# Attention between two expert layers: one stack of keys for both passes, fewer scratch transfers, and another order of the work beside the passes

## Chip, cores and metric

One core of a Trainium2 chip runs the whole program as one launch. The metric is the device time in microseconds. TensorE (PE) multiplies matrices, VectorE (DVE), ScalarE (ACT) and GpSimd (POOL) work on tiles, and SyncE (SP) issues the transfers (DMA) between SBUF and DRAM. Each engine works through its own instructions in order and meets the others at semaphores.

## The reference, cut to what matters

Sixteen sequences of 512 rows and 128 features go through three layers: half of a top-2-of-8 expert layer, attention, half of the expert layer again. Only attention changes.

```python
def attention(x):                       # x: layer norm of the stream, [16, 512, 128]
    q, k, v = ((x @ W + b).reshape(16, 512, 16, 8) for W, b in ((Wq, bq), (Wk, bk), (Wv, bv)))
    scores = einsum('bthd,bshd->bhts', q, k) / sqrt(8)
    scores += slope[h] * -abs(s - t)     # alibi
    scores = where(s > t, -inf, scores)  # causal
    out = einsum('bhts,bshd->bthd', softmax(scores), v)
    return out.reshape(16, 512, 128) @ Wo + bo
```

## The kernel before

`macaron` runs `moe_layer`, `attention` and `moe_layer` one after the other, with the stream x resident in SBUF.

**Steps, groups and units.** In `attention` every engine runs `step(b)` for b from -3 to 16, and each step is a `walk` over 4 groups g of 11 units n, written (g, n) here. A step works on several sequences at once. In each unit TensorE makes scores of sequence b+1 for its row maxima (`take_max_scores`, units 0 to 10, L895 and L898), and transposed scores of sequence b for the exponentials (`take_exp_scores`, units 0 to 9, L917). VectorE reduces the former (L1104), ScalarE exponentiates the latter (L997), POOL masks the diagonal blocks (L1069), and after the units of `PV_AFTER` TensorE multiplies the values with the group before (`weigh_values`, L933). Both kinds of scores go through rings of 3 PSUM tiles, so that TensorE is at most three units ahead of VectorE and of ScalarE.

**Side work.** `SIDE_WORK` says after which unit TensorE puts a piece in that is needed once a sequence: `turn_h` (transposes of the normalised rows, of b+2), `project_q` and `project_k` (of b+2), `project_v` (of b+1), `shift_lo` and `shift_hi` (a transpose of the maxima), `turn_o0`, `turn_o1`, `turn_o` and `output`. All go through one PSUM tile, `side_ps`, so each waits until ScalarE or VectorE has read the piece before it. `PREPARE` places the rest: POOL's `split_q0` to `split_k3`, which take q and k apart into three bf16 parts, the layer norm's statistics, and the normalisation of b+3.

**The stacks.** One matmul with a height of up to 64 rows yields a score in full precision. It wants a stack: for each pair of heads, 6 products of parts x 8 features = 48 rows, then constant rows (3 for alibi; `FINE` rows, which mask inside a diagonal block of the maxima; a `FAR` row, which masks in the exponentials; a `SHIFT` row, which subtracts the row's maximum there). The even heads lie in partitions 0 to 63, the odd ones in 64 to 127, and a unit's two matmuls use one half each. There are a stack of q (`q_st`) and two of k (`k_max`, `k_exp`), which differ in their constant rows alone; each is doubled by the parity of the sequence.

**SyncE's order** in step b is written out in its `step`: `place_shift(b, 1)` puts the high half of the shift into `q_st`; `store_parts(b+2)` writes the parts to `scratch` in DRAM, a transfer for each of 6 products of q and of k (L835); `stack(b+2, 0)` waits until all of them have landed (L842) and half of the exponentials of b are made (L844), and reads the first half of the pairs back, for three stacks and two sides (L849); `place_shift(b+1, 0)`; and `stack(b+2, 1)`, which waits for the last exponentials of b. TensorE waits for the first half before unit (0, 0) of the maxima of the next step, and for the second before (2, 0); and for the shift's halves (L859) before (0, 0) and (2, 0) of the exponentials. Scratch holds a part as

```python
scratch = [parity, side, 6 products, 2 (even, odd head), HD, PAIRS, S]   # bf16, 128 KB a product
sp.dma_start(scratch[par, side, term].rearrange("u d r s -> r (u d) s"), parts[side][:, part])
```

The steps up to 1 and from 12 on are unrolled; those between are a loop of two.

## Time and profile before

| | |
|---|---|
| median of 3 runs | 1024.37 us (1023.14 to 1026.57) |
| the profiled execution's own time | 1028.07 us |
| its span, first to last instruction | 1026.4 us |
| granted TensorE clock, mean | 0.898 of 2.4 GHz |
| busy: PE, DVE, ACT, POOL | 844.9, 746.9, 639.1, 537.0 us |
| attention, from its first to its last matmul | about 171 to 861 us |

The profile is of one execution. An engine's busy time does not count its waits; a matmul's end is modelled, and matmuls overlap. A row of the windows gives each engine's busy time in one stretch, the granted clock (1.00 is 2.4 GHz, 0.50 is 1.2), the mean share of 16 DMA engines that were busy, and GB/s. A row of the timeline gives start, duration, instruction, and in brackets how long the engine was idle before it and what ended that.

### The profile page before, as it was taken

To read this page: it belongs to the slowest core of one execution; us is meant where nothing else is said; L and a number is where in the kernel's file an instruction comes from. 1 tells how busy PE (TensorE), PEld (TensorE's weight loads), DVE (VectorE), ACT (ScalarE), POOL (GpSimd) and SP (SyncE) were. 2 spreads that over 40 slices of the span, in tenths; PEclk is the share of its full clock that TensorE was granted. 3 is DMA by queue.
4 is the path that set the end of the run, shared out by engine and by line. 5 is a ranking of instruction groups with operands and counts; after the bars stand their busy time and mean duration, and the time that the engine had idled before them with its cause. 6 is when DMAs were issued, how large, how long until landed. Compare 5 with 4: busy or idle time off the path is not lost. (4 is left out here: it accounts for less than half of the span.)

```text
span 1026.4 us, 24158 instructions
## 1 busy us (share of the span) xinstructions
PE 844.9 (82%) x6498; PEld 397.3 (39%) x6498; DVE 746.9 (73%) x2534; ACT 639.1 (62%) x1538; POOL 537.0 (52%) x838
## 2 busy tenths in 40 slices
PE   4999996198898898799788878988987985999997
PEld 3444442043343343334334434433433423544443
DVE  4899995278686776767767866876866902899996
ACT  2767674106576676676666766776765773676765
POOL 3777775234364463553552643653643331677777
PEclk9999998557898898988988989989988997999999
DMA  6600000332322322322323223223223000011001
GB/s 164 99 0 0 0 0 1 106 124 96 137 77 87 137 78 91 121 95 92 108 87 113 96 86 126 87 87 134 84 83 134 13 1 21 12 31 31 23 29 42
DMA packets 61436, 75.25 MB, mean 73 GB/s; under 512 B 8084, under 2 KB 51988, under 8 KB 61204
## 3 DMA queue, kind: packets, MB, share of 16 engines
q1 hardware_dynamic: 61384, 74.61, 22.5%
q8 instruction: 26, 0.43, 0.2%
q14 instruction: 26, 0.21, 0.1%
HBM read 44.97 MB, written 29.36 MB: 72 GB/s over the span
## 5 line engine op out<-in xcount | busy, mean ns | idle before, releaser
L1104 DVE TENSOR_REDUCE att_neg_max<-att_max 128x1 bf16<-128x512 f32 (+3 forms) x704 | 411.5, 636 | 171.5 <-PE att_max L898 169.8
L997 ACT ACTIVATE att_probs<-att_exp 128x512 f32<-128x512 f32 x640 | 349.4, 598 | 188.3 <-PE att_exp L917 184.8
L1069 POOL TENSOR_SCALAR_AFFINE_SELECT att_probs<-att_probs 128x512 f32<-128x512 f32 x256 | 157.4, 637 | 316.8 <-ACT att_probs L997 316.8
L895 PE MATMUL att_max<-att_k_max,att_q_st 51*128 51x384 bf16 (+2 forms) x768 | 191.1, 300 | 99.3 <-DMA att_k_exp<-qk_parts 78.0
L917 PE MATMUL att_exp<-att_q_st,att_k_exp 64*128 64x512 bf16 (+3 forms) x1024 | 217.4, 321 | 4.0 <-DMA att_q_st<-att_shift 2.1
L933 PE MATMUL att_pv<-att_probs,att_v 128*32 128x512 f32 (+3 forms) x2048 | 207.2, 478 | 15.8 <-POOL att_probs L1069 15.8
L358 ACT ACTIVATE moe_scaled<-moe_hi,moe_gates 128x128 f32<-128x128 f32 x512 | 146.1, 372 | 61.2 <-PE moe_hi L304 60.9
L895 PEld LDWEIGHTS att_max<-att_k_max,att_q_st 51*128 51x128 bf16 x768 | 73.8, 98 | 281.6 <-DVE att_neg_max L1104 148.4
L898 PE MATMUL att_max<-att_k_max,att_q_st 62*128 62x128 bf16 x1024 | 178.2, 231 | 0.0
L518 DVE SCALAR_TENSOR_TENSOR x<-moe_lo,moe_gates,x 128x128 f32 (+1 forms) x512 | 160.6, 338 | 20.1 <-PE moe_lo L298 18.9
L298 PE MATMUL moe_lo<-moe_we,moe_hT 128*128 128x512 f32 x256 | 136.0, 613 | 0.0
L304 PE MATMUL moe_hi<-moe_we,moe_hT 128*128 128x512 f32 x256 | 135.2, 610 | 0.0
L395 POOL TENSOR_TENSOR moe_part<-moe_scaled 128x256 f32<-128x256 f32 x128 | 93.4, 730 | 55.3 <-ACT moe_scaled L358 50.2
L898 PEld LDWEIGHTS att_max<-att_k_max,att_q_st 62*128 62x128 bf16 x1024 | 90.5, 99 | 12.0 <-issue 11.7
L917 PEld LDWEIGHTS att_exp<-att_q_st,att_k_exp 64*128 64x128 bf16 x1024 | 70.5, 96 | 25.9 <-ACT att_probs L997 14.5
L933 PEld LDWEIGHTS att_pv<-att_probs,att_v 128*32 128x32 f32 x2048 | 42.1, 111 | 71.3 <-issue 48.3
L304 PEld LDWEIGHTS moe_hi<-moe_we,moe_hT 128*128 128x128 f32 x256 | 47.1, 193 | 48.5 <-issue 48.5
L409 POOL TENSOR_TENSOR x<-x,moe_part 128x128 f32 (+1 forms) x128 | 58.8, 460 | 12.6 <-DVE x L518 12.4
L336 ACT ACTIVATE moe_hn<-x,moe_nmr,moe_rstd 128x128 f32 (+1 forms) x128 | 52.7, 498 | 17.5 <-DVE moe_nmr L452 17.5
L402 POOL TENSOR_TENSOR moe_part<-moe_part 128x128 f32<-128x128 f32 x128 | 58.5, 457 | 0.2
L298 PEld LDWEIGHTS moe_lo<-moe_we,moe_hT 128*128 128x128 f32 x256 | 44.9, 195 | 33.1 <-issue 24.9
L388 POOL TENSOR_TENSOR moe_rstd<-moe_veps,f_consts 128x4 f32<-128x4 f32 x32 | 32.6, 1020 | 37.8 <-DVE moe_veps L447 35.8
(81 smaller groups left out, 879.1 us busy)
## 6 DMA issues: line engine op xcount, KB each, us to landing
qk_parts<-att_parts SPq DMA_DIRECT2D x192, 128.0 KB
att_q_st<-qk_parts SPq DMA_DIRECT2D x64, 192.0 KB
att_k_max<-qk_parts SPq DMA_DIRECT2D x64, 192.0 KB
att_k_exp<-qk_parts SPq DMA_DIRECT2D x64, 192.0 KB
x<-in_L_attn_x SPq DMA_DIRECT2D x16, 256.0 KB, 2.9
out<-x SPq DMA_DIRECT2D x16, 256.0 KB, 2.3
moe_we<-in_L_ffn_We SPq DMA_DIRECT2D x2, 512.0 KB, 4.7
att_q_st<-att_shift SPq DMA_DIRECT2D x64, 4.0 KB, 2.1
```

The lines of the kernel that those rows point to most:

```text
L298: nc.tensor.matmul(lo_ps[t][:], hT[par][:, t * P:(t + 1) * P], we[:, 0:HE, :], start=True, stop=True).then_inc(lo_out, 1)
L304: nc.tensor.matmul(hi_ps[t % 2][:], hT[par][:, t * P:(t + 1) * P], we[:, HE:E, :], start=True, stop=True).then_inc(hi_out, 1)
L358: ins = nc.scalar.activation(scaled[t % 2][:, e, :], hi_ps[t % 2][:, e, :], ACT.Copy, scale=gates[par][:, t, HE + e:HE + e + 1])
L395: nc.gpsimd.tensor_tensor(part2[t % 2][:], scaled[t % 2][:, 0:2, :], scaled[t % 2][:, 2:4, :], ALU.add).then_inc(part_step, 1)
L518: nc.vector.scalar_tensor_tensor(out=xt(b, t), in0=lo_ps[t][:, e, :], scalar=gates[par][:, t, e:e + 1], in1=xt(b, t), op0=ALU.mult, op1=AL ...
L895: nc.tensor.matmul(max_ps[m % RING][:, at:at + width - P], q_st[par][low:low + FINE_ROW, r, i * P:(i + 1) * P], k_max[par][low:low + FINE_ ...
L898: mm = nc.tensor.matmul(max_ps[m % RING][:, at + width - P:at + width], q_st[par][low:low + FAR_ROW, r, i * P:(i + 1) * P], k_max[par][low ...
L917: mm = nc.tensor.matmul(exp_ps[m % RING][:, c:c + S - j * P], k_exp[par][low:low + SIDE, r, j * P:(j + 1) * P], q_st[par][low:low + SIDE, ...
L933: mm = nc.tensor.matmul(pv_ps[VW * hh:VW * (hh + 1), j * P:S], v[par][:, j, 4 * half_at + hh, ab, :], probs[g % 2][:, n, c:c + S - j * P], ...
L997: nc.scalar.activation(probs[g % 2][:, n, :], exp_ps[m % RING][:], ACT.Exp).then_inc(exp_done, 1)
L1069: nc.gpsimd.affine_select(out=view, in_=view, compare_op=ALU.is_ge, fill=0.0, base=0, pattern=[[0, 4], [1, P]], channel_multiplier=-1).the ...
L1104: nc.vector.tensor_reduce(neg_max[par][:, g // 2, 1 - g % 2, heads[0]:heads[0] + len(heads), i], max_ps[m % RING][:, 0:len(heads) * width] ...
```

## The change

- One stack of k, `k_st`, takes the place of `k_max` and `k_exp`. Its constant rows are reordered (alibi, far, shift, fine). The maxima's diagonal blocks use all 64 rows, their other blocks the first 51; the exponentials use the first 53.
- Because the maxima now also see the shift row of `q_st`, `stack` writes zeros there (`no_shift`, 8 KB) before the shift is known, once for each half.
- Products that share a part are stored by one transfer, which reads the part 2 or 3 times: three transfers for q and three for k. The columns of Wq, bq, Wk and bk are put in the order (even or odd, feature, pair) on the host, so that a part's 128 partitions are one contiguous block of `scratch`.
- A half of the shift, for both sides of `q_st`, is placed by one transfer.
- `stack` waits for the store of q before q's transfers and for the store of k before k's.
- `SIDE_WORK` and `PREPARE` are laid out anew: q and k are projected and split in group 0 and at the head of group 1; the statistics and most of the normalisation stand in group 2 (`NORMALISE`), and `turn_h` transposes sequence b+3 at (3, 8), where before b+2 was transposed at (0, 3) of the next step.

```diff
@@ -30,16 +30,17 @@
-K_PARTS = [0, 1, 2, 0, 1, 0]
+K_PARTS = [1, 0, 2, 0, 1, 0]
+PART_TERMS = [[slice(0, 3), slice(3, 5), slice(5, 6)], [slice(1, 6, 2), slice(0, 5, 4), slice(2, 3)]]
...
-FINE_ROW = ALIBI_ROW + 3
+FAR_ROW = ALIBI_ROW + 3
+SHIFT_ROW = FAR_ROW + 1
+FINE_ROW = SHIFT_ROW + 1
...
-FAR_ROW = FINE_ROW + FINES
-SHIFT_ROW = FAR_ROW + 1
...
-assert SHIFT_ROW + 1 == SIDE
+assert FINE_ROW + FINES == SIDE
@@ -108,20 +109,21 @@
-        self.k_max_rows, self.k_exp_rows = [], []
+        fine_at, far_at = FINE_ROW - ALIBI_ROW, FAR_ROW - ALIBI_ROW
+        self.k_rows = []
...
+            rows[far_at] = bf16_parts(k_far, 1)[0]
...
-            rows[FAR_ROW - ALIBI_ROW] = bf16_parts(k_far, 1)[0]
-            self.k_exp_rows.append(nc.inline_tensor(rows, f"k_exp_rows_{ab}").ap().bitcast(BF16))
-            rows = rows[:FAR_ROW - ALIBI_ROW].copy()
-            rows[3:] = bf16_parts(k_fine, 1)[0][:, None]
-            self.k_max_rows.append(nc.inline_tensor(rows, f"k_max_rows_{ab}").ap().bitcast(BF16))
-        rows = np.full((SHIFT_ROW - ALIBI_ROW, PAIRS, S), one, np.uint16)
-        rows[FINE_ROW - ALIBI_ROW:FAR_ROW - ALIBI_ROW] = bf16_parts(q_fine, 1)[0][:, None]
-        rows[FAR_ROW - ALIBI_ROW] = bf16_parts(q_far, 1)[0]
+            rows[fine_at:] = bf16_parts(k_fine, 1)[0][:, None]
+            self.k_rows.append(nc.inline_tensor(rows, f"k_rows_{ab}").ap().bitcast(BF16))
+        rows = np.full((SIDE - ALIBI_ROW, PAIRS, S), one, np.uint16)
+        rows[far_at] = bf16_parts(q_far, 1)[0]
+        rows[SHIFT_ROW - ALIBI_ROW] = 0
+        rows[fine_at:] = bf16_parts(q_fine, 1)[0][:, None]
...
+        self.no_shift = nc.inline_tensor(np.zeros((2, PAIRS // 2, S), np.uint16), "no_shift").ap().bitcast(BF16)
@@ -562,17 +564,17 @@
-    {3: "turn_h", 7: "project_q"},
-    {0: "project_k", 5: "shift_hi", 9: "turn_o1"},
-    {3: "turn_o", 7: "shift_lo"},
-    {0: "project_v", 4: "output", 9: "turn_o0"},
+    {2: "project_q", 4: "shift_hi", 8: "project_k"},
+    {1: "turn_o1", 6: "project_v"},
+    {1: "turn_o", 6: "shift_lo", 10: "output"},
+    {1: "turn_o0", 8: "turn_h"},
...
-PREPARE = {(0, 10): "split_q0", (1, 0): "split_q1", (1, 1): "split_q2", (1, 2): "split_q3",
-           (1, 3): "split_k0", (1, 4): "split_k1", (1, 5): "split_k2", (1, 6): "split_k3", (2, 4): "add_bias",
-           (3, 0): "statistics", (3, 1): "aggregate", (3, 2): "add_eps", (3, 3): "take_root", (3, 6): "shift_mean",
-           (3, 7): "normalise0", (3, 8): "normalise1", (3, 9): "normalise2", (3, 10): "normalise3"}
+PREPARE = {(0, 5): "split_q0", (0, 6): "split_q1", (0, 7): "split_q2", (0, 8): "split_q3",
+           (0, 10): "split_k0", (1, 0): "split_k1", (1, 1): "split_k2", (1, 2): "split_k3", (2, 5): "add_bias"}
+NORMALISE = {(2, 0): "statistics", (2, 1): "aggregate", (2, 2): "add_eps", (2, 3): "take_root", (2, 7): "shift_mean",
+             (2, 8): "normalise0", (2, 9): "normalise1", (2, 10): "normalise2", (3, 0): "normalise3"}
@@ -712,9 +710,9 @@
-        SCRATCH_DMAS = len(Q_PARTS)
-        STACK_DMAS = 6
-        SHIFT_DMAS = 2
+        SCRATCH_DMAS = 3
+        STACK_DMAS = 5
+        SHIFT_DMAS = 1
@@ -784,11 +779,10 @@
                         on_exp(b, par, half, g, n)
-                    if on_prepare and (g, n) in PREPARE:
-                        if g < GROUPS - 1 and there(b + 2):
-                            on_prepare(b + 2, par, half + 1, PREPARE[g, n])
-                        if g == GROUPS - 1 and there(b + 3):
-                            on_prepare(b + 3, 1 - par, half + par + 1, PREPARE[g, n])
+                    if on_prepare and (g, n) in PREPARE and there(b + 2):
+                        on_prepare(b + 2, par, half + 1, PREPARE[g, n])
+                    if on_prepare and (g, n) in NORMALISE and there(b + 3):
+                        on_prepare(b + 3, 1 - par, half + par + 1, NORMALISE[g, n])
@@ -828,36 +822,32 @@
-                which = (Q_PARTS, K_PARTS)[side]
-                for term in sorted(range(len(which)), key=lambda t: which[t]):
-                    part = which[term]
+                for part, terms in enumerate(PART_TERMS[side]):
                     sp.wait_ge(split_step[side], b * 4 + (1, 3, 4)[part])
-                    sp.dma_start(scratch[par, side, term].rearrange("u d r s -> r (u d) s"),
-                                 parts[side][:, part]).then_inc(scratch_in[par][side], DMA)
+                    dst = scratch[par, side, terms].rearrange("t u d r s -> (u d r) t s")
+                    sp.dma_start(dst, parts[side][:, part].unsqueeze(1).to_broadcast(list(dst.shape))).then_inc(
+                        scratch_in[par][side], DMA)
...
-                if hf == 0:
-                    for side in range(2):
-                        sp.wait_ge(scratch_in[par][side], half * (SCRATCH_DMAS * DMA) + SCRATCH_DMAS * DMA)
+                pairs = slice(hf * PAIRS // 2, (hf + 1) * PAIRS // 2)
                 if after(b, 1):
                     sp.wait_ge(exp_out, (b - 2) * NE + (hf + 1) * NE // 2)
-                pairs = slice(hf * PAIRS // 2, (hf + 1) * PAIRS // 2)
-                for side, stacks in ((0, (q_st,)), (1, (k_max, k_exp))):
-                    for dst in stacks:
-                        for ab in range(2):
-                            sp.dma_start(dst[par][ab * SIDE:ab * SIDE + HEAD_ROWS, pairs, :],
-                                         scratch[par, side, :, ab, :, pairs]).then_inc(
-                                stack_in[par][hf], DMA)
+                sp.dma_start(q_st[par][SHIFT_ROW:SHIFT_ROW + SIDE + 1:SIDE, pairs, :],
+                             consts.no_shift).then_inc(stack_in[par][hf], DMA)
+                for side, dst in enumerate((q_st[par], k_st[par])):
+                    if hf == 0:
+                        sp.wait_ge(scratch_in[par][side], half * (SCRATCH_DMAS * DMA) + SCRATCH_DMAS * DMA)
+                    for ab in range(2):
+                        sp.dma_start(dst[ab * SIDE:ab * SIDE + HEAD_ROWS, pairs, :],
+                                     scratch[par, side, :, ab, :, pairs]).then_inc(stack_in[par][hf], DMA)
...
                 pairs = slice(hf * PAIRS // 2, (hf + 1) * PAIRS // 2)
-                for ab in range(2):
-                    rows = PAIRS // 2 * T
-                    sp.dma_start(q_st[par][ab * SIDE + SHIFT_ROW:ab * SIDE + SHIFT_ROW + 1, pairs, :],
-                                 shift[ab * rows:(ab + 1) * rows, :]).then_inc(shift_in[par][hf], DMA)
+                sp.dma_start(q_st[par][SHIFT_ROW:SHIFT_ROW + SIDE + 1:SIDE, pairs, :],
+                             shift[:]).then_inc(shift_in[par][hf], DMA)
@@ -893,11 +883,11 @@
                         nc.tensor.matmul(max_ps[m % RING][:, at:at + width - P],
-                                         q_st[par][low:low + FINE_ROW, r, i * P:(i + 1) * P],
-                                         k_max[par][low:low + FINE_ROW, r, 0:width - P], start=True, stop=True)
+                                         q_st[par][low:low + FAR_ROW, r, i * P:(i + 1) * P],
+                                         k_st[par][low:low + FAR_ROW, r, 0:width - P], start=True, stop=True)
                     mm = nc.tensor.matmul(max_ps[m % RING][:, at + width - P:at + width],
-                                          q_st[par][low:low + FAR_ROW, r, i * P:(i + 1) * P],
-                                          k_max[par][low:low + FAR_ROW, r, width - P:width], start=True, stop=True)
+                                          q_st[par][low:low + SIDE, r, i * P:(i + 1) * P],
+                                          k_st[par][low:low + SIDE, r, width - P:width], start=True, stop=True)
@@ -915,8 +905,8 @@
                     mm = nc.tensor.matmul(exp_ps[m % RING][:, c:c + S - j * P],
-                                          k_exp[par][low:low + SIDE, r, j * P:(j + 1) * P],
-                                          q_st[par][low:low + SIDE, r, j * P:S], start=True, stop=True)
+                                          k_st[par][low:low + FINE_ROW, r, j * P:(j + 1) * P],
+                                          q_st[par][low:low + FINE_ROW, r, j * P:S], start=True, stop=True)
@@ -1013,7 +1003,7 @@
-                    nc.scalar.activation(hT[par][:], side_ps[:], ACT.Copy).then_inc(side_read, 1)
+                    nc.scalar.activation(hT[1 - par][:], side_ps[:], ACT.Copy).then_inc(side_read, 1)
@@ -1040,7 +1030,7 @@
                     if after(b, 0):
-                        act.wait_ge(turned, use(b - 3, "turn_h"))
+                        act.wait_ge(turned, use(b - 4, "turn_h"))
@@ -1187,6 +1177,10 @@
+    for n in ("Wq", "bq", "Wk", "bk"):
+        a = arrays[f"in_L0_attn_{n}"]
+        by_side = a.reshape(-1, PAIRS, 2, HD).transpose(0, 2, 3, 1)
+        arrays[f"in_L0_attn_{n}"] = np.ascontiguousarray(by_side).reshape(a.shape)
```

## Rows read from the trace of the kernel before

**Rows 1.** Windows by step: the columns are each engine's busy time, PEclk, DMA share, GB/s

```profile
206.60:238.00 31.40, 28.64 (x129) 13.12 (x129) 26.47 (x55) 3.88 (x8) 9.33 (x10) 0.50 0.36 125
238.00:275.70 37.70, 30.29 (x295) 13.29 (x296) 27.62 (x57) 25.06 (x50) 19.07 (x26) 0.86 0.31 108
275.70:315.70 40.00, 33.12 (x343) 14.82 (x344) 28.96 (x60) 26.59 (x52) 19.06 (x26) 0.88 0.29 99
...
749.80:790.20 40.40, 33.35 (x342) 14.73 (x342) 27.97 (x50) 25.19 (x48) 18.00 (x25) 0.88 0.29 97
790.20:821.00 30.80, 29.21 (x330) 12.94 (x330) 26.35 (x47) 23.17 (x45) 8.86 (x15) 0.94 0.10 37
```

**Rows 2.** The waits, whole span: us in total, times, longest us

```profile
PE att_max L895 <- DMA att_k_exp<-qk_parts: 78.0, 16, 23.1
```

**Rows 3.** Timeline of TensorE: start, us, instruction, [idle before it and what ended it]

```profile
473.41 0.49 PE L895 MATMUL att_max<-att_k_max,att_q_st 51*128 51x384 bf16 x1 [2.11 <-DMA att_k_exp<-qk_parts]
...
495.28 1.06 PE L933 MATMUL att_pv<-att_probs,att_v 128*32 128x512 f32 x8 [0.91 <-POOL att_probs L1069]
...
836.05 0.82 PE L917 MATMUL att_exp<-att_q_st,att_k_exp 64*128 64x512 bf16 x3 [2.06 <-DMA att_q_st<-att_shift]
```

**Rows 4.** Timeline of SyncE's DMA queue in the prologue and one step

```profile
194.66 1.56 SPq L849 DMA_DIRECT2D att_q_st<-qk_parts  x2
...
449.23 1.20 SPq L859 DMA_DIRECT2D att_q_st<-att_shift  x2
450.56 8.08 SPq L835 DMA_DIRECT2D qk_parts<-att_parts  x12
462.00 1.52 SPq L849 DMA_DIRECT2D att_q_st<-qk_parts  x2
...
470.10 1.54 SPq L849 DMA_DIRECT2D att_q_st<-qk_parts  x2
```

**Rows 5.** Windows in which stores move (first) and stacks move (second)

```profile
183.50:192.50 9.00, 0.06 (x1) 0.00 (x0) 5.38 (x14) 1.78 (x4) 4.79 (x5) 0.50 0.51 165
...
464.00:480.50 16.50, 13.96 (x121) 5.88 (x116) 11.84 (x29) 9.96 (x20) 4.15 (x6) 0.79 0.38 140
```

**Rows 6.** Windows by group: two of the step from 434.9, three of the next

```profile
444.30:451.50 7.20, 7.20 (x82) 3.08 (x79) 6.64 (x12) 6.79 (x14) 6.20 (x8) 1.00 0.01 1
451.50:461.90 10.40, 8.59 (x89) 3.45 (x85) 6.70 (x14) 5.91 (x13) 6.31 (x10) 0.84 0.47 151
...
473.40:484.60 11.20, 11.19 (x86) 4.61 (x87) 5.96 (x11) 6.90 (x13) 1.99 (x4) 0.70 0.23 90
...
492.30:500.70 8.40, 6.95 (x81) 3.31 (x82) 6.31 (x12) 6.17 (x14) 6.15 (x9) 1.00 0.52 171
500.70:514.20 13.50, 8.20 (x94) 4.40 (x92) 9.65 (x26) 6.94 (x15) 3.93 (x6) 0.87 0.30 102
```

**Rows 7.** Timeline of TensorE: side work in the step from 434.9

```profile
444.72 1.12 PE L948 MATMUL att_side<-att_hT,att_wk 128*128 128x512 f32 x2
...
450.58 0.66 PE L972 MATMUL att_side<-f_consts,att_oT 128*128 128x128 f32 x4
...
462.31 1.16 PE L952 MATMUL att_side<-att_wv,att_hT 128*128 128x128 f32 x8
```

**Rows 8.** Part 5 of the page

```profile
L1104 DVE TENSOR_REDUCE att_neg_max<-att_max 128x1 bf16<-128x512 f32 (+3 forms) x704 | 411.5, 636 | 171.5 <-PE att_max L898 169.8
```

**Rows 9.** Timeline of VectorE: k's last split, the statistics

```profile
187.86 0.69 DVE L824 TENSOR_TENSOR att_parts<-att_rest,att_parts 128x512 bf16<-128x512 f32 x1
...
501.59 0.86 DVE L1115 BATCH_NORM_STATS2 att_bn<-x 128x6 f32 x4
```

**Rows 10.** Timeline of POOL: the splits and four masks

```profile
485.07 0.62 POOL L814 TENSOR_SCALAR att_parts<-att_qk 128x512 bf16<-128x512 f32 x1
485.77 1.16 POOL L817 TENSOR_TENSOR att_rest<-att_qk,att_parts 128x512 f32<-128x512 f32 x1
...
493.42 2.40 POOL L1069 TENSOR_SCALAR_AFFINE_SELECT att_probs<-att_probs 128x512 f32<-128x512 f32 x4
```

More of the change, by code:

```diff
@@ L620, in __init__ @@
         self.v_set = ctx.enter_context(nc.semaphore("att_v_set"))
[L621 removed]
+        self.N_WEIGHTS, self.N_ROWS, self.N_V = 8 * DMA, 8 * DMA, 6
     def load(self, eng):
@@ L743, in attention @@
         L = len(order)
-        before = {-2: 0}
-        for n in range(-1, 3):
-            before[n] = before[n - 1] + sum(present(n - 1, what) for what in order)
-        before[NSEQ - 2] = before[2] + (NSEQ - 4) * L
-        for n in range(NSEQ - 1, NSEQ + 2):
+        before = {-3: 0}
+        for n in range(-2, NSEQ + 2):
             before[n] = before[n - 1] + sum(present(n - 1, what) for what in order)
@@ L753, in use @@
             here = order[:order.index(what) + 1]
-            if isinstance(b, int) and b in before:
+            if isinstance(b, int):
                 return before[b] + sum(present(b, w) for w in here)
```

17 lines of the change are left out of this document (6 added, 11 removed).

## The prediction

> **What bounds the kernel now.** I read the page first, then the windows by step, the waits, SyncE's queue, and last the four groups inside one step. The page gives attention some 650 of 1026 us. The windows cut it into the steps that TensorE walks [rows 1]: in each, the maxima of sequence b+1, the exponentials of b and the values of b are interleaved. Thirteen steps in steady state run from 275.7 to 790.2, that is 39.6 us each, of which VectorE is busy 29, ScalarE 26.6, POOL 19. No engine fills a step.
>
> The waits say where the rest goes. TensorE stands at the first maximum of a step until the stack has come from DRAM: 16 times, 78.0 us together, the longest 23.1 [rows 2]. The 23.1 is the prologue; the other 15 are 54.9 us, 3.7 a step. Behind each such wait the clock is at its lower level: the first group after it runs 11.2 us at a granted 0.70, while a group with no wait in it takes 7.2 us at 1.00, all of it busy [rows 3, 6]. The group before it holds two more losses: TensorE stands 0.91 us for POOL's masks [rows 3], and the fourth group takes 8.6 us before the wait even starts, because VectorE has 9.65 us of work there and may lag by three units at most [rows 6].
>
> Why the stack is late is to be read in SyncE's queue [rows 4]. In the step that begins at 434.9 the stores of sequence b+2 are issued at 450.6, because they stand behind the shift's placement (449.2), and that behind a transpose scheduled in the second group. Twelve stores; the stack's first transfer goes out only when all have landed, at 462.0; its six transfers arrive at 473.4, 38.5 us after the step's start. While stacks move, the DMA engines are busy for 0.38 of 16 and move 140 GB/s, stores 0.51 and 165 GB/s [rows 5]: a stack transfer of 192 KB takes 1.4 us, and nothing issued faster helps it.
>
> **The change part by part.**
>
> *The chain of transfers.* project_q goes from (group 0, unit 7) to (0, 2), project_k from (1, 0) to (0, 8), the shift from (1, 5) to (0, 4), the splits from (0, 10)..(1, 6) to (0, 5)..(1, 2). With a unit at about 0.7 us, q is projected by 2 us, k by 7 us. POOL needs 2 x (0.62 + 1.16) = 3.6 us for a split, and 2.4 us for a group's four masks [rows 10]. In order: mask, q0 to q2 until 7.0, two masks, q3 to 9.7, a mask, k0 to k3 until 14.0. The last store goes out at 14 and lands by about 17 (POOL's last split to stack's first issue took 194.66 - 188.6 = 6 us in the prologue with twelve stores queued [rows 4, 9]; with that whole delay it is 20). The stack's first half also waits for half of the exponentials of b, at about 15.5 us. It is now four transfers of 192 KB plus one zero row, not six: 4 x 1.4 = 5.5 us of data and the 3.1 us that the old six showed over their 8.2 (473.4 - 462.0 = 11.4). It lands at 25 to 29 us, and the next step starts after 31. The 3.7 us wait goes in all 15 steps, with 3 to 6 us to spare. I count it as gone.
>
> *The second half.* It waits for the last exponential, at about 30 us, as now at 470.1 [rows 4]; five issues and 8.6 us later it lands 8 us into the next step, where it is wanted at 15. The zeroed shift row is issued ahead of its four transfers and adds some 0.6 us to SyncE's queue; the shift's own placement saves one issue twice a step. Both are covered by these margins. The placement of the high shift now queues behind this half; it is wanted at 15 too.
>
> *TensorE's work* is the same, laid out otherwise. From the 7.2 us group [rows 6], which holds a projection (1.12), four transposes (0.66) and a shift transpose (0.2, by a fourth of the 0.66) [rows 7], 5.2 us are maxima, exponentials and values. The new groups: 5.2 + 1.1 + 0.2 + 1.1 = 7.7; 5.2 + 0.66 + 1.16 = 7.0; 5.2 + 0.66 + 0.2 + 1.16 = 7.2; 5.2 + 2 x 0.66 = 6.5. One stack of keys changes the height of the maxima's and exponentials' operands (51, 62 and 64 rows to 51, 64 and 53), not their columns; both halves still lie in 64 rows, so I cost it at nothing. If pairs of heads no longer ran side by side, it would show at once as 0.2 us a unit.
>
> *VectorE.* 704 maxima take 411.5 us, 6.4 a group; the 3.3 us left of its 29 are two turns of the output, the copy of v, the output's add and the statistics (0.86, and an estimated 0.4 for what follows them) [rows 1, 8, 9]. Before, copy, add, statistics and one turn all fell in the fourth group. Now: 6.4, 7.6, 8.1, 7.0.
>
> *The step.* TensorE sets the first group (7.7). Then VectorE does: 22.7 for the other three, against 20.7 for TensorE. Sum 30.4. For friction I add 1.1: the values of group 0 come at about 9.3 us, and POOL, with q's split ahead of their last mask, is through at 10.3. The floor is VectorE's 29.0; the ceiling is the old step less its wait, 39.6 - 3.7 = 35.9. I take 31.5, near the floor, because the busy group at full clock is the nearest row and its four together make 28.4.
>
> *The sum*, against the profiled execution's own 1028.1 us:
> - 13 steps of 39.6 to 31.5: -105
> - the step from 238.0, 37.7 to 31.5: -6.2
> - the step from 790.2, 30.8, whose first group also starts at the lower clock: VectorE's order gives about 28.3: -2.5
> - the first step, 31.4, which ends in such a wait: half an average one, -2
> - the last exponentials' wait for the shift, 2.06 [rows 3]: -2, as it is placed 12 units sooner
> - the prologue: k's last split ends at 188.6 [rows 9]. At the stores' old rate (165 GB/s from 183.5 [rows 5]) 1.5 MB are through at 193 and landed at 194.7 as before; q's stack is moved meanwhile, k's two transfers take 2.8 + 3.1 us: the first maximum at 200.6, not 206.6: -6 (bounds: 0 if the halves get in each other's way, -9 if stores are faster)
>
> That is -123.7. The medians lie 3.7 under the profiled time, so 1024.4 - 123.7 = 900.7; I say 901.
>
> By the Trainium skill, "DMA: Bandwidth & Descriptors", section "Why a DMA increments its semaphore by 16 and not by 1", a transfer runs on the largest number of engines up to 16 that divides the slowest dimension of both sides. The trace agrees where it can: stores with a slowest dimension of 8 keep 0.51 of the engines busy, stacks with 6 keep 0.38. The rule would put the new stores, 128 on both sides, on all 16: the prologue's -6 would be -8, 899 in all, and the stacks stay at six engines.
>
> **The rivals.**
> 1. *The wait goes, the step does not fall so far* (0.25). The steps keep a hole where TensorE waits for POOL or for VectorE's add of the output at (2, 10), which the turn at (3, 1) needs. For it: in the step shown, 0.91 us of waiting sat in a group of 8.4 us whose work is 6.1 (5.2, four transposes and the shift's). Where such a hole also drops the clock, as in the third group of the step from 434.9 (10.4 us at 0.84), another 2 us go [rows 3, 6]. 33 to 35.5 us a step: 922 to 957.
> 2. *Nothing but VectorE* (0.06): 29 to 30.2 us a step, 866 to 882.
> 3. *Part of the wait stays* (0.05): POOL's splits are pushed back by masks until the stack lands after 31.5 us. Against it: 2.5 us to spare even with the long landing. Each us late is 15 us: 915 to 1000.
> 4. *No change* (0.01): the wait only moves to the second half at (2, 0), which is issued when the first used to be wanted. It would need 7 us more than I give it, then the old 8 us again.
> 5. *Slower* (0.03), by the same place: the second half is not issued before the last exponential, and everything behind it in SyncE's queue (high shift, q's stores) waits. If the five issues and their data took over 23 us instead of 8.6, TensorE would stand more than 8 us at (2, 0), and a step would be longer than 39.6; at 26 us the time is 1047. Nothing in rows 5 shows a transfer at a third of its rate.
>
> **How the numbers follow.** The forecast (0.60) has 30.2 to 33 us a step: 14 steps x 1.3 below and 1.5 above 31.5, 883 to 922. For eight in ten I add the nearer half of rival 1 and the upper edge of rival 2: 880 to 940. Faster by over 0.3% (about what a measurement of this kernel can tell): 0.60 + 0.25 + 0.06 + 0.05 = 0.96; within 0.3%: 0.01; slower: 0.03.
>
> **What would show it.** In the changed profile TensorE's wait for a stack transfer at a step's head is gone, and PEclk shows nines through attention. SyncE issues the first stack about 16 us into a step. The steps are 31 to 32 us, POOL's masks end one of TensorE's waits in the second group, not the third. The prediction is wrong if the first group is over 8.5 us at full clock (the coupling of side work and copies is dearer than its sum), if a wait stands at (2, 0), or if single maxima and exponentials no longer overlap.

## The result, and the profile after

The changed kernel takes 933.6 us (median of four runs, 930.7 to 948.3) against 1023.8 for the kernel before on the same chip: a ratio of 0.911, 95% interval 0.907 to 0.915, so about 90 us or 8.9% faster. Some executions fall into a slower state of the chip (here the one of 948.3): the medians of this document take them in, the ratios and their intervals leave them out. The forecast was 901, its range 880 to 940. The profiled execution took 934.8 us, with a span of 933.1.

The steps first, in the windows of the changed kernel (same columns as [rows 1]): the first step, the one after it, the thirteen of the steady state together, one of them, and the last one with maxima.

```profile
198.00:230.00 32.00, 29.17 (x131) 12.72 (x132) 26.16 (x55) 3.88 (x8) 9.33 (x10) 0.50 0.33 118
230.00:265.80 35.80, 31.80 (x295) 12.87 (x293) 27.74 (x58) 25.48 (x50) 18.46 (x25) 0.86 0.20 69
265.80:701.70 435.90, 418.08 (x4442) 184.72 (x4442) 381.88 (x771) 345.16 (x671) 247.88 (x338) 1.00 0.28 96
...
434.10:467.80 33.70, 32.36 (x344) 14.35 (x342) 29.47 (x61) 26.68 (x52) 19.12 (x27) 1.00 0.28 94
...
701.70:732.00 30.30, 29.17 (x335) 13.00 (x336) 27.86 (x51) 23.37 (x45) 9.77 (x17) 1.00 0.09 29
```

Thirteen steps take 435.9 us where they took 514.5: 33.5 each for 39.6, TensorE's clock at 1.00. The prologue ends 8.6 us earlier (198.0 for 206.6). The first step is 0.6 longer (32.0 for 31.4), the next 1.9 shorter (35.8 for 37.7), the last 0.5 shorter (30.3 for 30.8). From the span's start to this point that is 89.0 us; what follows gives 4.3 more, among it the last exponentials' wait for the shift, 2.06 us before, which is gone.

The waits of the changed kernel (us in total, times, longest us) answer to [rows 2]. (PEld is TensorE's loading of weights.) The fourth line is that of the kernel before which answers to the third:

```profile
PE att_max L885 <- DMA att_k_st<-qk_parts: 4.1, 1, 4.1
...
PE att_pv L923 <- POOL att_probs L1059: 2.4, 2, 1.5
...
PEld att_max L885 <- DVE att_neg_max L1094: 159.1, 315, 1.5
...
PEld att_max L895 <- DVE att_neg_max L1104: 148.4, 225, 2.3
```

One wait of TensorE for a stack is left, in the prologue, 4.1 us for 23.1. POOL's masks cost 2.4 us in two waits. What is left is the wait for VectorE's reduction, through the ring of three: the loading of the next maximum's weights stood idle 159.1 us in 315 places, most of it covered by matmuls still running (the matmuls themselves waited 11.4 us in 35 places). This wait is not new; it was 148.4 us in 225 places before.

SyncE's queue in the step from 434.1 (start, us, instruction) answers to [rows 4]:

```profile
438.65 0.59 SPq L849 DMA_DIRECT2D att_q_st<-att_shift  x1
439.40 9.21 SPq L828 DMA_DIRECT2D qk_parts<-att_parts  x6
450.15 0.53 SPq L836 DMA_DIRECT2D att_q_st<-no_shift  x1
450.83 1.50 SPq L842 DMA_DIRECT2D att_q_st<-qk_parts  x2
452.38 1.41 SPq L842 DMA_DIRECT2D att_k_st<-qk_parts  x2
...
466.76 0.52 SPq L836 DMA_DIRECT2D att_q_st<-no_shift  x1
```

The stores begin 5 us into the step and the last is issued by 14.5; the stack's first half goes out at 16.1, where half of the exponentials are made. How soon it lands is read from the windows by group, which answer to [rows 6]:

```profile
434.10:443.00 8.90, 8.80 (x86) 3.27 (x84) 6.55 (x12) 6.99 (x14) 5.02 (x8) 1.00 0.39 133
443.00:451.50 8.50, 8.19 (x91) 3.90 (x88) 7.69 (x15) 6.02 (x12) 7.01 (x10) 1.00 0.40 141
451.50:460.20 8.70, 8.30 (x92) 3.94 (x89) 8.13 (x23) 7.31 (x16) 5.07 (x7) 1.00 0.28 91
460.20:467.80 7.60, 7.08 (x81) 3.23 (x81) 7.09 (x14) 6.35 (x13) 2.02 (x4) 1.00 0.00 0
```

In the fourth group the DMA engines are idle (0.00), so the half had landed by 460.2, 26 us into the step and 7.6 before it is wanted. The columns are TensorE, weight loads, VectorE, ScalarE and POOL. TensorE is the busiest engine in the first three groups (8.80, 8.19 and 8.30 us of 8.9, 8.5 and 8.7), VectorE a close second in the second and third (7.69 and 8.13); in the fourth they are level (7.08 and 7.09 of 7.6). TensorE's busy time is not a fixed amount of work, though: where its matmuls overlap better, the same ones fill less of it, as the experiments show.

### The profile page after: what moved, and what is told of

It reads as the page before. It is cut to its first block and busy times, and to the rows that moved or that the text cites. A ratio compares the mean times of both kernels' runs of the same rounds, so it can differ in the third digit from the quotient of the medians.

```text
span 933.1 us, 23978 instructions
## 1 busy us (share of the span) xinstructions
PE 828.5 (89%) x6498; PEld 383.2 (41%) x6498; DVE 752.8 (81%) x2534; ACT 640.4 (69%) x1538; POOL 537.4 (58%) x838
## 5 line engine op out<-in xcount | busy, mean ns | idle before, releaser
L987 ACT ACTIVATE att_probs<-att_exp 128x512 f32<-128x512 f32 x640 | 357.6, 596 | 102.4 <-PE att_exp L907 98.5
L907 PE MATMUL att_exp<-att_q_st,att_k_st 53*128 53x512 bf16 (+3 forms) x1024 | 223.0, 302 | 0.6 <-ACT att_probs L987 0.6
L885 PE MATMUL att_max<-att_k_st,att_q_st 51*128 51x384 bf16 (+2 forms) x768 | 191.2, 285 | 19.4 <-DVE att_neg_max L1094 11.4
L923 PE MATMUL att_pv<-att_probs,att_v 128*32 128x512 f32 (+3 forms) x2048 | 191.8, 448 | 2.7 <-POOL att_probs L1059 2.4
L888 PE MATMUL att_max<-att_k_st,att_q_st 64*128 64x128 bf16 x1024 | 176.0, 224 | 0.0
L885 PEld LDWEIGHTS att_max<-att_k_st,att_q_st 51*128 51x128 bf16 x768 | 71.1, 95 | 216.4 <-DVE att_neg_max L1094 159.1
L888 PEld LDWEIGHTS att_max<-att_k_st,att_q_st 64*128 64x128 bf16 x1024 | 87.9, 97 | 12.1 <-issue 11.7
L907 PEld LDWEIGHTS att_exp<-att_q_st,att_k_st 53*128 53x128 bf16 x1024 | 65.2, 94 | 11.7 <-ACT att_probs L987 8.6
L300 PEld LDWEIGHTS moe_lo<-moe_we,moe_hT 128*128 128x128 f32 x256 | 44.9, 195 | 32.8 <-issue 24.7
L390 POOL TENSOR_TENSOR moe_rstd<-moe_veps,f_consts 128x4 f32<-128x4 f32 x32 | 32.5, 1016 | 37.6 <-DVE moe_veps L449 35.6
```

Of the source, the lines that this page charges most:

```text
L300: nc.tensor.matmul(lo_ps[t][:], hT[par][:, t * P:(t + 1) * P], we[:, 0:HE, :], start=True, stop=True).then_inc(lo_out, 1)
L885: nc.tensor.matmul(max_ps[m % RING][:, at:at + width - P], q_st[par][low:low + FAR_ROW, r, i * P:(i + 1) * P], k_st[par][low:low + FAR_ROW ...
L888: mm = nc.tensor.matmul(max_ps[m % RING][:, at + width - P:at + width], q_st[par][low:low + SIDE, r, i * P:(i + 1) * P], k_st[par][low:low ...
L907: mm = nc.tensor.matmul(exp_ps[m % RING][:, c:c + S - j * P], k_st[par][low:low + FINE_ROW, r, j * P:(j + 1) * P], q_st[par][low:low + FIN ...
L923: mm = nc.tensor.matmul(pv_ps[VW * hh:VW * (hh + 1), j * P:S], v[par][:, j, 4 * half_at + hh, ab, :], probs[g % 2][:, n, c:c + S - j * P], ...
L987: nc.scalar.activation(probs[g % 2][:, n, :], exp_ps[m % RING][:], ACT.Exp).then_inc(exp_done, 1)
```

## The experiments

All are compared with the kernel before on their own chip. Groups are counted from VectorE's first reduction of a group to that of the next, in the regular steps of the loop (with the transfers only, in those that no clock drop lengthens); the step is their sum.

| kernel | us, median | ratio (95%) | groups of a steady step | step |
|---|---|---|---|---|
| changed | 933.6 | 0.911 (0.907 to 0.915) | 8.98 8.40 8.71 7.61 | 33.7 |
| changed, again | 935.4 | 0.910 (0.906 to 0.915) | 8.98 8.40 8.71 7.61 | 33.7 |
| transfers only | 949.2 | 0.925 (0.917 to 0.932) | 8.47 7.60 8.43 9.39 | 33.9 |
| order only | 942.0 | 0.916 (0.909 to 0.924) | 8.98 8.40 8.71 7.61 | 33.7 |
| statistics early | 923.9 | 0.897 (0.890 to 0.905) | 8.98 8.40 8.02 7.62 | 33.0 |
| early, output in group 3 | 928.6 | 0.904 (0.896 to 0.911) | 8.98 8.40 7.09 8.99 | 33.5 |
| pieces ahead of values | 934.0 | 0.909 (0.905 to 0.912) | 8.74 8.50 8.38 8.00 | 33.6 |
| the same, early | 933.5 | 0.907 (0.904 to 0.911) | 8.80 8.50 8.28 8.00 | 33.6 |
| pieces in the gap | 918.2 | 0.894 (0.891 to 0.897) | 8.20 8.30 8.71 7.61 | 32.8 |
| in the gap, early | 911.8 | 0.888 (0.885 to 0.891) | 8.36 8.13 8.15 7.61 | 32.3 |
| twelve wide stores | 932.3 | 0.907 (0.900 to 0.915) | 8.98 8.40 8.71 7.61 | 33.7 |
| half projections | 938.8, one run | | 8.15 8.63 8.71 7.61 | 33.1 |
| short reductions | 917.6, one run | | 8.34 8.21 8.72 7.51 | 32.8 |

**1. Transfers only, and order only.** The first is the changed kernel with `SIDE_WORK`, `PREPARE` and the place of `turn_h` as before; the second the kernel before with the new ones. The core of the first's edit (the second's is its inverse):

```diff
-    {2: "project_q", 4: "shift_hi", 8: "project_k"},
-    {1: "turn_o1", 6: "project_v"},
-    {1: "turn_o", 6: "shift_lo", 10: "output"},
-    {1: "turn_o0", 8: "turn_h"},
+    {3: "turn_h", 7: "project_q"},
+    {0: "project_k", 5: "shift_hi", 9: "turn_o1"},
+    {3: "turn_o", 7: "shift_lo"},
+    {0: "project_v", 4: "output", 9: "turn_o0"},
```

> The changed kernel's transfers (one key stack, six stores, zero row, single shift placement, wait for q and k apart) in the old order of side work. Theory A (either half of the change alone takes the wait at the step's head away, because six fewer-byte transfers end well before the step does): k's last split still ends about 19 us into a step, its store lands at 21 to 22, k's two stack transfers at 28 to 30, the step is 33 to 34.5 us (groups of 8.5, 7.6, 8.4 and 9 at full clock), the time 930 to 950. Theory B (the order is what removes it): TensorE still waits 2 us or more a step, the clock drops behind it, the step stays over 36 and the time over 965.

> The new order of side work with the old transfers (two key stacks, twelve stores, two shift placements). Theory A: splits end about 15 us into a step, the twelve stores land at about 20, the six stack transfers take 11.4 and land at 31 to 32, under the 33.7 us of the changed kernel's step: no wait, or under 1 us. Prologue as before (8 us longer than in the changed kernel). Time 940 to 955. Theory B' (the transfers are what removes it): 3 us of wait a step with the clock behind it, over 970.

Measured: 949.2 and 942.0. Either half by itself takes the wait at the steps' heads away (with the order alone one of 15 is left, 0.98 us before the last step with maxima); the gains do not add. With the order alone the steady step is the changed kernel's to 0.01 us in every group, so there the new transfers are worth nothing. With the transfers alone, waits and windows of that kernel read:

```profile
PE att_pv L927 <- POOL att_probs L1063: 15.9, 15, 2.6
PE att_max L889 <- DMA att_k_st<-qk_parts: 15.7, 1, 15.7
```

```profile
434.90:468.80 33.90, 31.10 (x342) 14.67 (x342) 28.96 (x62) 26.52 (x53) 19.09 (x26) 1.00 0.27 94
468.80:505.40 36.60, 33.83 (x342) 15.16 (x342) 28.93 (x61) 26.53 (x53) 19.14 (x26) 0.91 0.26 87
```

A quiet step takes 33.9 us. In the old order TensorE still meets POOL's masks in every step (15 waits, 15.9 us; 0.9 us in a regular one), and nine of the thirteen steps stay at full clock in spite of it. In the other four the clock falls at that wait, and the third group is 1.6 to 2.8 us longer: 11.2 us at a granted 0.69 in the step from 468.8, which takes 36.6. So it is the lower clock behind the wait, not the wait, that sets these four apart; why it falls in some steps and not in others, no run here shows. The thirteen take 448.2 us (265.6 to 713.8) where the changed kernel's take 435.9, which is most of the 16 us between the two.

The difference between order alone and the changed kernel, 8 us, lies in the prologue: the first maximum comes at 206.3, not 198.0. SyncE's queue with the order alone:

```profile
182.20 8.05 SPq L831 DMA_DIRECT2D qk_parts<-att_parts  x12
194.28 1.56 SPq L845 DMA_DIRECT2D att_q_st<-qk_parts  x2
```

and in the changed kernel:

```profile
181.71 5.75 SPq L828 DMA_DIRECT2D qk_parts<-att_parts  x6
...
188.19 1.56 SPq L842 DMA_DIRECT2D att_q_st<-qk_parts  x2
```

**2. Which edit shortens the prologue.** The changed kernel with a store for each product, still in blocks of 128 rows:

```diff
-                    dst = scratch[par, side, terms].rearrange("t u d r s -> (u d r) t s")
-                    sp.dma_start(dst, parts[side][:, part].unsqueeze(1).to_broadcast(list(dst.shape))).then_inc(
-                        scratch_in[par][side], DMA)
+                    for term in range(len(Q_PARTS))[terms]:
+                        sp.dma_start(scratch[par, side, term].rearrange("u d r s -> (u d r) s"),
+                                     parts[side][:, part]).then_inc(scratch_in[par][side], DMA)
```

> The changed kernel, but every product is stored by a transfer of its own again: twelve stores of 128 KB in place of six, each still one contiguous block of 128 rows in scratch. Theory H (the prologue's 8.3 us come from the stores' layout: with 128 rows on both sides they use more of the DMA engines and land sooner after their issue; the number of stores costs only its issues): the share of busy DMA engines between 182 and 189 us stays well above the 0.40 of the kernel with twelve stores in the old layout (0.64 in the changed one), the twelve issues take 8 us in place of 5.75, the first stack goes out about 2.5 us later than in the changed kernel, and the first maximum is at 200.5 to 202 (changed kernel 198.0, old layout 206.9). Rival (it is the number of transfers, or reading a part once for several products): a share of 0.40 to 0.45 and a first maximum at 204 to 207. The steady steps stay at 33.7 by both, and the time is 934 to 938 by Theory H, 938 to 943 by the rival.

Windows and SyncE's queue of this kernel:

```profile
182.00:189.00 7.00, 0.00 (x0) 0.00 (x0) 5.33 (x14) 0.09 (x1) 3.40 (x3) 0.50 0.53 176
```

```profile
179.61 6.82 SPq L828 DMA_DIRECT2D qk_parts<-att_parts  x12
...
187.16 1.56 SPq L842 DMA_DIRECT2D att_q_st<-qk_parts  x2
188.76 1.41 SPq L842 DMA_DIRECT2D att_k_st<-qk_parts  x2
```

The same window of the order alone, and of the changed kernel:

```profile
182.00:189.00 7.00, 1.41 (x2) 0.00 (x0) 4.31 (x13) 0.69 (x1) 3.36 (x4) 0.50 0.40 127
```

```profile
182.00:189.00 7.00, 0.92 (x2) 0.00 (x0) 4.40 (x13) 0.69 (x1) 3.27 (x4) 0.50 0.64 226
```

These three windows do not compare like with like: with the order alone and in the changed kernel the first store is issued at 182.20 and 181.71, so that some 2 us of the window pass before data flow, with twelve wide stores at 179.61. Windows of 2 us in which the most data moved, for the order alone, twelve wide stores and the changed kernel:

```profile
188.00:190.00 2.00, 0.00 (x0) 0.00 (x0) 0.91 (x7) 0.00 (x0) 0.83 (x1) 0.50 0.54 178
...
185.00:187.00 2.00, 0.00 (x0) 0.00 (x0) 1.33 (x9) 0.00 (x0) 0.41 (x1) 0.50 0.77 265
...
187.00:189.00 2.00, 0.00 (x0) 0.00 (x0) 1.42 (x10) 0.00 (x0) 0.32 (x1) 0.50 0.97 338
```

From 184 to 192 the old layout stands at 0.51 to 0.54 in every 2 us; the new one reaches 0.97. By the Trainium skill, "DMA: Bandwidth & Descriptors", "Why a DMA increments its semaphore by 16 and not by 1", a slowest dimension of 128 takes 16 engines and one of 8 takes eight; the rows agree in kind.

The expert layer ahead ends at times that differ by some 2.5 us between kernels, so the path is counted from the end of k's last split to the first maximum: 18.7 us with the order alone (187.6 to 206.3), 10.9 in the changed kernel (187.1 to 198.0), 11.8 with twelve wide stores (185.0 to 196.8). The kernel before has 18.1 and the transfers alone 10.7, so the transfers shorten it and not the order. Their number is worth 0.9 us, less than the 2.5 to 4 that Theory H gave it; the other kernels with the changed kernel's six stores lie between 9.6 and 11.5, so 0.9 is hardly clear of their spread. The rival, that the number or the repeated reading of a part makes the prologue's gain, falls.

The 6.9 us that are left are not the stores' layout alone, since the order alone also has six stack transfers for four and waits for both stores before the first of them. The queues divide them. From the last split to the first stack transfer it is 6.7 us (194.28) and with twelve wide stores 2.2 (187.16); from there to the first maximum 12.0 and 9.6. The latter 2.4 us go with the stack of k that is no longer read, two transfers of 1.41 us together. Of the former 4.5, at least 2.9 belong to the layout: with twelve wide stores k's transfers follow q's without a gap at 188.76, so that all stores had landed by 3.8 us after the split, where it took 6.7. The remaining 1.6 us or less are what q's transfers gain by going out before k's stores have landed. This division is worked out from the queues; no run changes one of the three alone.

**3. Which engine sets a group.** Three edits that move or take away work of one engine. Statistics early:

```diff
-NORMALISE = {(2, 0): "statistics", (2, 1): "aggregate", (2, 2): "add_eps", (2, 3): "take_root", (2, 7): "shift_mean",
+NORMALISE = {(0, 4): "statistics", (0, 6): "aggregate", (0, 9): "add_eps", (2, 3): "take_root", (2, 7): "shift_mean",
```

> The changed kernel with the statistics, their aggregate and the eps moved from (2, 0), (2, 1), (2, 2) to (0, 4), (0, 6), (0, 9), where VectorE stands dry behind the projections. Theory C (the step of 33.7 is a sum of groups of which TensorE sets the first and VectorE the others, and the ring of three cannot carry idle time from one to the next): the third group loses about 1.1 us and the first stays at 9.0 to 9.2, step 32.5 to 32.9, time 917 to 925. Theory D (TensorE's own work and its switches between kinds of matmul set all groups): no change within 0.3 us a step, 930 to 936.

Early, and the output moved as well (`output` from (2, 10) to (3, 5)):

> As e3, and the output projection moved from (2, 10) to (3, 5), so that VectorE's add no longer stands between (2, 10) and the turn at (3, 1). Theory C: another 0.3 to 0.6 us off a step, 32.0 to 32.5, time 910 to 920. Theory D: as the changed kernel, 930 to 936.

Half projections multiplies q and k for 256 of 512 rows; short reductions takes the maximum of the last unit of a group over 32 keys:

```diff
-                    mm = nc.tensor.matmul(side_ps[:], w["wq" if what == "project_q" else "wk"][:], hT[par][:],
+                    mm = nc.tensor.matmul(side_ps[:, 0:S // 2], w["wq" if what == "project_q" else "wk"][:], hT[par][:, 0:S // 2],
...
+                part = 32 if n == MAX_UNITS - 1 else width
```

> The changed kernel with project_q and project_k computing only the first 256 of 512 rows: half of q and k stays what the tile held before, so scores of the second half of the rows are wrong; every transfer, split and copy keeps its size. TensorE's side work in the first group falls by 1.1 us. Theory C (TensorE sets the first group, VectorE the others): the first group goes from 8.98 to 7.8 to 8.0 us, the others stay within 0.2, step 32.5 to 32.8, profiled span 915 to 920. Theory E (VectorE's ring and ScalarE's copies set the first group too): it stays above 8.6, span over 927.

> The changed kernel with VectorE's maximum of unit 10 taken over the first 32 keys of each of the four heads, 128 columns instead of 512 (the maxima of the first 128 rows of a sequence are too small, the exponentials there larger). VectorE has 0.4 us less in each group. Theory C: the second, third and fourth group lose 0.3 to 0.4 us each, the first 0 to 0.2 (it starts behind VectorE's lag), step 32.4 to 32.8, span 915 to 921. Theory D (TensorE's own work sets all groups): within 0.3 us of 33.7, span over 928.

Measured: the 0.73 us of VectorE's work that leaves the third group shorten it by 0.69, and cost the first nothing: 33.0 a step, 923.9 us. Moving the output takes 0.93 more from the third and puts 1.37 on the fourth; 928.6, where less than 920 was expected. With 1.12 us less of TensorE's work in the first group that group loses 0.83 and the second gains 0.23. With 0.4 us less of VectorE's in each group the step loses 0.9, but 0.64 of it in the first group, where TensorE was the fuller engine, and nothing in the third. So the step answers to both engines: 0.6 us for 1.12 of TensorE's, 0.9 for VectorE's 1.6 by count, 1.2 by its busy time (29.47 to 28.27).

Why the short reductions left the third group as it was is to be seen at its end, where VectorE's last reductions are followed by its add of the output. The changed kernel first, then short reductions:

```profile
457.67 1.89 DVE L1094 TENSOR_REDUCE att_neg_max<-att_max 128x2 bf16<-128x512 f32 x3 [0.33 <-PE att_max L888]
459.79 0.69 DVE L1136 TENSOR_TENSOR x<-att_side,x 128x512 f32 x1 [0.24 <-PE att_side L956]
```

```profile
480.23 1.49 DVE L1095 TENSOR_REDUCE att_neg_max<-att_max 128x2 bf16<-128x512 f32 x3
482.36 0.69 DVE L1138 TENSOR_TENSOR x<-att_side,x 128x512 f32 x1 [0.64 <-PE att_side L956]
```

The reductions end 0.40 us sooner, and the add waits 0.40 longer for TensorE's output projection: there the group's end hangs on TensorE. With the output moved away this group fell to 7.09.

**4. Where the pieces stand in a group.** First, pieces moved right ahead of a group of values, with and without the statistics early (`project_q` at 3, `project_k` at 9, `project_v` at 7, and so on), to spare TensorE's changes between scores and other work:

> The changed kernel with each piece of side work put right ahead of a piece of the values, in the same unit (q at (0, 3), high shift at (0, 5), k at (0, 9), the turns at (1, 3), (2, 3), (3, 3), v at (1, 7), low shift at (2, 7), output at (2, 9), turn of h at (3, 7)), so that TensorE goes from the passes' matmuls to others 4 times a group and not 6 or 7. A single unit ahead of a piece took 0.32 us, one ahead of a unit 0.22 to 0.23. Theory F (each going over costs TensorE 0.1 to 0.15 us, and that is part of what the sum lacked): the first group loses 0.3 to 0.4 us, the others up to 0.2, step 32.8 to 33.3, time 920 to 929. Theory C alone (clumps matter, not the number of switches): longer clumps starve VectorE more, step 33.7 to 34.5, time 933 to 946.

> e7 with the statistics at (0, 4), (0, 6), (0, 9) as in e3. Theories C and F together: 0.7 us less than e7 in the third group, step 32.1 to 32.6, time 908 to 918. If e7 brings nothing by itself: as e3, 921 to 926.

Both 934: that theory falls. The first group is 0.24 us shorter, but the fourth 0.39 longer, and the early statistics, worth 0.69 us in the changed kernel's third group, are worth 0.10 here. Waits of TensorE's matmuls for the reductions were more, not fewer (24.7 us in 72 places against 11.4 in 35).

Then the opposite. The values stand after units 3, 5, 7 and 9; at the end and start of a group TensorE has only short units, and by Theory G could run ahead of VectorE but for the ring (of the pieces that the expectation lists, the turned half of the output stays at (1, 1); the splits of k move too):

```diff
-    {2: "project_q", 4: "shift_hi", 8: "project_k"},
-    {1: "turn_o1", 6: "project_v"},
+    {0: "project_q", 4: "shift_hi", 10: "project_k"},
+    {1: "turn_o1", 10: "project_v"},
...
-           (0, 10): "split_k0", (1, 0): "split_k1", (1, 1): "split_k2", (1, 2): "split_k3", (2, 5): "add_bias"}
+           (1, 1): "split_k0", (1, 2): "split_k1", (1, 4): "split_k2", (1, 5): "split_k3", (2, 5): "add_bias"}
```

> The changed kernel with the same side pieces, the large ones (query projection, key projection, turned half of the output, value projection) moved to the first unit of their group or to its last, beside which no values are issued; the preparation of the next sequence's queries and keys moved one unit later where it needs to be. Theory G (the values follow only in the middle of a group, so at its end and start TensorE could emit several short units while VectorE is still at its reductions, and is held there by the ring of three; a large piece put there costs neither engine anything): a steady step takes 32.5 us or less in place of 33.7, waits of TensorE for VectorE in the ring fall, and the kernel takes 912 to 922. Rival (the step is the sum of the two engines' work with its queues' friction wherever the pieces stand, as the run with the pieces ahead of the values suggested): the step within 0.3 us of 33.7 and the kernel 929 to 938.

> The run with the large pieces at the groups' ends, and the statistics of the query-key norm moved into the first group as in the earlier run (which gave 923.9). Theory G: both add up, a step of 31.5 to 32.2 us, the kernel 900 to 913. Rival: no more than the early statistics alone give, 921 to 927.

> The changed kernel itself once more, so that the two others are compared with it on the same chip: every theory expects 930 to 936, and a steady step of 33.6 to 33.8.

Windows of the kernel with the pieces in the gap, its first two groups and the whole step:

```profile
424.90:433.10 8.20, 8.20 (x84) 3.18 (x84) 6.37 (x12) 6.82 (x14) 4.69 (x8) 1.00 0.43 137
433.10:441.40 8.30, 7.78 (x91) 3.90 (x88) 7.63 (x15) 5.95 (x12) 7.37 (x10) 1.00 0.43 151
...
424.90:457.70 32.80, 31.30 (x343) 14.35 (x344) 29.32 (x61) 26.43 (x52) 19.04 (x27) 1.00 0.29 97
```

The first group has the same side pieces as in the changed kernel and takes 8.2 us for 8.9, TensorE being busy 8.20 for 8.80, and VectorE runs dry less. VectorE's timeline over the same stretch, the changed kernel first (start, us, instruction, [idle before it and its end]):

```profile
436.56 0.69 DVE L1094 TENSOR_REDUCE att_neg_max<-att_max 128x1 bf16<-128x512 f32 x1 [0.38 <-PE att_max L888]
437.83 1.05 DVE L1094 TENSOR_REDUCE att_neg_max<-att_max 128x1 bf16<-128x384 f32 x2 [0.57 <-PE att_max L888]
439.42 1.02 DVE L1094 TENSOR_REDUCE att_neg_max<-att_max 128x1 bf16<-128x384 f32 x2 [0.55 <-PE att_max L888]
440.60 0.69 DVE L1094 TENSOR_REDUCE att_neg_max<-att_max 128x2 bf16<-128x512 f32 x1 [0.15 <-PE att_max L888]
441.99 1.98 DVE L1094 TENSOR_REDUCE att_neg_max<-att_max 128x2 bf16<-128x512 f32 x3 [0.70 <-PE att_max L888]
```

```profile
426.31 2.82 DVE L1094 TENSOR_REDUCE att_neg_max<-att_max 128x1 bf16<-128x512 f32 x5 [0.77 <-PE att_max L888]
429.62 1.02 DVE L1094 TENSOR_REDUCE att_neg_max<-att_max 128x1 bf16<-128x384 f32 x2 [0.49 <-PE att_max L888]
430.80 1.89 DVE L1094 TENSOR_REDUCE att_neg_max<-att_max 128x2 bf16<-128x512 f32 x3 [0.15 <-PE att_max L888]
433.10 1.29 DVE L1094 TENSOR_REDUCE att_neg_max<-att_max 128x1 bf16<-128x512 f32 x2 [0.41 <-PE att_max L888]
```

2.35 us of waits in the changed kernel's five rows, 1.82 in the other's four. A step takes 32.8 us rather than 32.5 or less, because the second group gained only 0.1, but the time, 918.2, is in Theory G's range, and 17 us under the changed kernel's on the same chip. That the place of the pieces matters is shown; that it matters by Theory G's mechanism is not. The waits that it names hardly fell: those of the weight loads from 159.1 to 154.5 us, those of the matmuls from 11.4 to 8.3. What fell is TensorE's own busy time, from 32.36 to 31.30 us a step for the same matmuls, so they overlap better; why, no run shows. With the statistics early too it is 911.8, a step of 32.3 (31.5 to 32.2 expected): a ratio of 0.888 for the changed kernel's 0.910 on the same chip, 2.4% less, and the fastest of all. The whole step of that kernel:

```profile
421.00:453.30 32.30, 31.12 (x343) 14.44 (x344) 29.80 (x62) 26.30 (x52) 19.02 (x27) 1.00 0.28 98
```

TensorE is busy 31.1 of its 32.3 us and VectorE 29.8, so little is left to gain unless TensorE's busy time falls further.

## Why the prediction was right, and by how much it missed

**The wait at the steps' heads.** Right in mechanism, place and size: gone in all fifteen steps, the last store issued by 14.5 us (14 said), the stack's first half issued at 16.1 (15.5), landed by 26 (25 to 29). But it was not the chain's shortening as a whole that was needed; either half of the change would have done, but for 0.98 us once.

**The step.** The term that was mis-sized is "Sum 30.4. For friction I add 1.1 ... I take 31.5": it measured 33.7 in the profile's regular steps, 33.5 on average. VectorE's work was counted well: its 7.6, 8.1 and 7.0 us of the last three groups measured 7.69, 8.13 and 7.09. TensorE's was not: 7.7, 7.0, 7.2 and 6.5, together 28.4, were said, and it was busy 8.80, 8.19, 8.30 and 7.08, together 32.4. So the step that failed is "Then VectorE does", which lets VectorE set three groups by itself, with TensorE's 20.7 us hidden under it. What was missing is what the two engines lose to each other:
- the first group, 7.7 said, 8.98 measured: 1.3
- the other three over VectorE's busy time in them: 0.7, 0.6 and 0.5, so 1.8
- the friction given, 1.1, was laid to POOL's masks in the second group. In the steady step there was none; that wait stood only in the step from 230, once, 1 us. The place was wrong, and the amount had nothing to do with it.

That the ring of three is what makes them lose it is an argument: no run changed its length. Shown is that the step shortens when either engine is relieved (experiment 3).

The first group's 1.3 has two parts. "5.2 us are maxima, exponentials and values" came from a window of 7.2 us, 444.3 to 451.5, which is not a whole group. From reduction to reduction that group takes 7.60 in ten of the thirteen steps of the kernel before and 7.52 in the other three, and 7.60 with the transfers alone; this gives 5.6, so 0.4 is a window drawn too short. The other 0.9 is where the projections stand: with them in the gap 0.8 of it comes back (8.2 measured). Where the prediction said what would prove it wrong, it named this: "the first group is over 8.5 us at full clock (the coupling of side work and copies is dearer than its sum)". That is what the profile showed.

**The sum.** Between the spans' start and the last step with maxima:
- thirteen steps: -105 said, -78.6 measured
- the step from 238.0: -6.2 said, -1.9 measured (37.7 to 35.8); its second group, 11.8 us, holds the mask wait and a lower clock
- the last: -2.5 said, -0.5 measured
- the first: -2 said, +0.6 measured
- the prologue: -6 said, -8.6 measured, 1.5 of which is the expert layer ending earlier, and 7.1 the path from k's last split. That it came near is two errors against each other: from k's last split 6.1 us were given to the stores' landing and 5.9 to k's transfers; it took 2.7 at most until k's stores had landed (189.80) and 8.2 from there. By the rule of the Trainium skill it was -8, 0.9 us from the 7.1, where -6 is 1.1 from it.
- the last exponentials' wait: -2 said, and gone

The time came out 33 us over the 901 of the sum, 26 of them from the thirteen steps. The time is that of rival 1, *the wait goes, the step does not fall so far* (33 to 35.5 us a step, 922 to 957), which had 0.25; its price was right. Of its causes a hole at POOL's masks was wrong; at the output's add there is one, but of 0.24 us. The forecast's own band, 883 to 922, which had 0.60, was missed; 933.6 lies in the range of 880 to 940 because half of rival 1 was added to it. So the range held by what the rivals were given, and the forecast's working for the step did not.

## What to carry to other kernels

A stage in which two engines work in step through a short ring does not take the longer of their counted works: here each of the last three groups took 0.5 to 0.7 us more than VectorE's busy time, and relieving either engine gave back a part of what was taken away, 0.6 us for 1.12 and 0.9 for 1.2 to 1.6. Before costing a move at "its duration, hidden", try where it stands: the same pieces moved by two to four units gave 17 us here. Before taking a base from a window, check that it spans a whole group: 0.4 us of the first group was missed so. When two edits each shorten one chain that has a fixed deadline, try each alone: here, with the new order in place, the new transfers bought only the prologue.

## What the runs showed of the hardware

- The layout of a store matters more than the number of stores: twelve stores of 128 KB with 128 rows on both sides were issued in 6.82 us (8.05 in the old layout, whose slowest dimension is 8) and kept up to 0.77 of the DMA engines busy in 2 us, at 265 GB/s, where the old layout never came over 0.54 and 178; six stores with 128 rows reached 0.97 and 338.
- A wait of 0.9 us of TensorE for POOL in the same place of every step, with the transfers alone, was followed by a lower clock in four of thirteen steps and not in nine.
- In the half projections' kernel the last step of attention, exponentials and values alone, ran at half the clock from end to end, where the changed kernel's ran at full. Its windows:

```profile
716.00:718.00 2.00, 1.35 (x16) 0.52 (x8) 1.48 (x3) 1.45 (x4) 1.53 (x3) 1.00 0.00 0
718.00:720.00 2.00, 2.00 (x9) 0.18 (x9) 0.00 (x0) 1.34 (x3) 0.49 (x1) 0.59 0.00 0
...
718.00:758.00 40.00, 40.00 (x190) 11.74 (x190) 2.25 (x5) 20.81 (x40) 8.12 (x13) 0.50 0.01 1
```

and the changed kernel's:

```profile
730.00:732.00 2.00, 1.61 (x33) 0.92 (x26) 1.85 (x5) 1.73 (x4) 1.19 (x3) 1.00 0.00 0
732.00:734.00 2.00, 1.74 (x12) 0.39 (x12) 0.57 (x1) 1.64 (x4) 0.61 (x2) 1.00 0.00 0
...
732.00:762.00 30.00, 27.22 (x245) 10.07 (x245) 2.82 (x6) 22.98 (x45) 10.39 (x18) 1.00 0.01 1
```

TensorE was idle for 0.65 us in the two microseconds ahead of it in the one, and for 0.65 us across the same place in the other (0.39 and 0.26), and only the first lost its clock. The half projections' kernel was 15 us ahead of the changed kernel at the start of this step, and took 4 us more in the end. Nothing in the two timelines tells them apart; its single time is no measure of the edit for that reason.
